# The fourth silu behind the next superstep's first two copies, and one weight tile 384 bytes further on

## The reference, cut to what matters

```python
g = jnp.einsum('bsh,ehf->ebsf', x, w_gate)      # x [2048, 256], e: 8 experts, f: 1024
u = jnp.einsum('bsh,ehf->ebsf', x, w_up)
h = jax.nn.silu(g) * u
expert_out = jnp.einsum('ebsf,efh->ebsh', h, w_down)
cw = router_probs * gate_weights                # softmaxes over the 8 experts
cw = cw / (jnp.sum(cw, axis=-1, keepdims=True) + 1e-09)
out = jnp.einsum('ebsh,bse->bsh', expert_out, cw)
```

## Time and profile before

| | us |
|---|---|
| median of 3 runs | 1723.94 |
| the three runs | 1719.41 to 1731.8 |
| the profiled execution, its own time | 1721.44 |
| its span, first to last instruction | 1719.6 |

### The profile page before, as it was taken

One profiled execution on the slowest core, in us unless ns is written; L12 is line 12 of the kernel. 1 busy time (PEld: TensorE's weight loads), 2 busy tenths in 40 slices (PEclk: granted clock), 3 DMA queues, 4 the chain that ended last, 5 costly groups with the idle time before them and its releaser, 6 DMA issues. The chain is left out here.

```text
span 1719.6 us, 25997 instructions
## 1 busy us (share of the span) xinstructions
PE 1578.9 (92%) x7985; PEld 1287.3 (75%) x7986; DVE 1205.1 (70%) x2226; ACT 874.0 (51%) x1548; POOL 665.8 (39%) x585
## 2 busy tenths in 40 slices
PE   6999986879993888889999999999999999999998
PEld 5796673368882777768888888778788788888787
DVE  6656878646665789567677777767767776876875
ACT  4455332134432456555665665665666655656653
POOL 2453156688806633330440530521612603604400
PEclk9998999889996999889999999999999999999999
DMA  6995012168843212000100100201101101101001
GB/s 198 264 328 207 13 69 93 62 211 260 253 138 112 80 36 74 1 1 27 56 31 31 56 13 31 68 0 49 49 0 49 49 1 56 42 12 55 31 13 50
DMA packets 74493, 136.38 MB, mean 79 GB/s; under 512 B 8592, under 2 KB 52176, under 8 KB 74256
## 3 DMA queue, kind: packets, MB, share of 16 engines
q1 hardware_dynamic: 40544, 92.76, 16.5%
q10 hardware_dynamic: 27696, 25.51, 4.8%
q0 software_dynamic: 6144, 16.79, 3.1%
HBM read 90.93 MB, written 44.11 MB: 79 GB/s over the span
## 5 line engine op out<-in xcount | busy, mean ns | idle before, releaser
L1356 DVE TENSOR_TENSOR gU<-ps,gU 128x512 f32<-128x512 f32 x384 | 256.7, 686 | 78.7 <-PE ps L2566 62.2
L2042 POOL TENSOR_TENSOR cL<-cR,cH 128x384 fp32r<-128x384 f32 x192 | 213.4, 1137 | 237.1 <-ACT cH L1734 237.1
L1349 DVE TENSOR_TENSOR eL<-eF,eH 128x512 fp32r<-128x512 f32 x256 | 190.0, 742 | 159.3 <-ACT eH L1829 159.3
L1813 ACT ACTIVATE gU<-ps 128x512 f32<-128x512 f32 x384 | 225.3, 596 | 124.4 <-PE ps L2566 110.1
L1829 ACT ACTIVATE eH<-eF 128x512 fp32r<-128x512 f32 x256 | 161.2, 630 | 162.9 <-DVE eF L1344 162.2
L2566 PE MATMUL ps<-xTH,cH 128*128 128x512 f32 x512 | 203.6, 398 | 10.2 <-DVE eF L1344 5.7
L2566 PE MATMUL ps<-xTL,cH 128*128 128x512 f32 x512 | 201.6, 394 | 0.0
L2566 PE MATMUL ps<-xTH,cL 128*128 128x512 f32 x512 | 201.4, 393 | 0.0
L2586 PE MATMUL ps<-eH,cL 128*128 128x512 f32 x480 | 189.1, 394 | 0.0
L2586 PE MATMUL ps<-eH,cH 128*128 128x512 f32 x480 | 188.5, 393 | 0.0
L2029 POOL TENSOR_TENSOR cR<-cR 128x256 f32<-128x256 f32 x32 | 34.1, 1064 | 395.2 <-DMA cR<-in_w 395.2
(11 more groups left out here) (439 smaller groups left out, 3447.3 us busy)
## 6 DMA issues: line engine op xcount, KB each, us to landing
cR<-in_w SPq DMA_DIRECT2D x32, 768.0 KB, 4.2
slots_in<-eS SPq DMA_DIRECT2D x16, 768.0 KB, 10.4
eS<-in_wr SPq DMA_DIRECT2D x32, 384.0 KB, 4.3
xl<-slots_in ACTq DMA_DIRECT2D x48, 256.0 KB, 3.8
slots_out<-yo ACTq DMA_DIRECT2D x48, 256.0 KB, 3.4
cwB<-expert_weights SPq DMA_DIRECT2D x16, 512.0 KB, 3.6
k_parts<-parts SPq DMA_DIRECT2D x8, 512.0 KB, 4.7
q_parts<-parts SPq DMA_DIRECT2D x8, 512.0 KB, 3.9
```

Source lines behind the costliest of these rows:

```text
L1349: dve.tensor_tensor(eL[:, b, :], eF[:, b, :], f32(eH[:, b, :]), ALU.subtract).then_inc(block_low, 1)
L1356: dve.tensor_tensor(to[:, :], ps[:, 2 + half, :], to[:, :], ALU.add).then_inc(half_summed, 1)
L1813: act.activation(to[:, :], ps[:, half, :], ACT.Identity).then_inc(snap_done, 1)
L2042: last = pool.tensor_tensor(cL[c][:, cols_], cR[c][:, cols_], f32(cH[c][:, cols_]), ALU.subtract)
```

## The change

In ScalarE's order the silu of the fourth inner block leaves the end of its superstep. It is issued in the next superstep, behind the two copies of k = 0 and right ahead of that block's `high_of`; behind the last superstep it stands alone. And `cH[3]` begins 384 bytes later, at byte 163840; it now reaches 384 bytes into `cw2`, and `cwc` moves to the second half of `cw2`. No instruction is added or removed.

```diff
-        cwc = at("cwc", [P, E1, NT], F32, start["cw2"])
+        cwc = at("cwc", [P, E1, NT], F32, start["cw2"] + 512)
...
-                                         (start["wS"] + 8 * CW, start["wS"] + 12 * CW), (start["sc0"], start["dcw"] + 8 * CW))):
+                                         (start["wS"] + 8 * CW, start["wS"] + 12 * CW), (start["sc0"] + 384, start["dcw"] + 8 * CW))):
...
-        assert end["cL2"] <= end["wL"] and end["cH3"] <= end["selm"] and end["cL0"] == start["cL3"]
+        assert end["cL2"] <= end["wL"] and end["cH3"] <= start["cwc"] and end["cwc"] <= end["cw2"] and end["cL0"] == start["cL3"]
...
+                before = (e, s - 1) if s else (e - 1, STEPS - 1)
                 snapshot(e, s, 0, 0)
                 snapshot(e, s, 0, 1)
                 if not start:
-                    high_of(*((e, s - 1) if s else (e - 1, STEPS - 1)), 3)
+                    gate(*before, 3)
+                    high_of(*before, 3)
...
                 high_of(e, s, 2)
                 if first and s == 2:
                     exponentials()
-                gate(e, s, 3)
...
             expert(E1 - 1, last=True)
+            gate(E1 - 1, STEPS - 1, 3)
             high_of(E1 - 1, STEPS - 1, 3)
```

## The result

The changed kernel takes 1731.91 us (median of 14 runs, 1727.75 to 1738.93) beside 1722.18 for the kernel before (14 runs, 1716.19 to 1731.8): a ratio of 1.0063, 95% interval 1.0046 to 1.008. It is slower by 0.6% where 5.6 us of gain were forecast, and it lies above the range of 1707 to 1728. Its profiled execution has a span of 1727.7 us, 8.1 more than that of before.

The account below looks back on a forecast made before the run. The prediction took TensorE's pace, and the few places where it waits, to bound the dense stage. Costs of 1.4 + 3.4 + 1.6 less a gain of 12.0 made minus 5.6, from 1721.44 to 1716 us, range 1707 to 1728.

Parts of the forecast that it names:

- (a): In 28 supersteps with a chunk, P7 waits for ScalarE's later copies of k = 1: 0.05 us each, 1.4 us.
- What comes: Part following the later silu: `hidden` 3 starts at about 2.75 us after the first matmul; three places have less slack.
- the loop's turn: VectorE's turn in superstep 0 of pass 6, after which `hidden` 3 came only at 2.68 us.
- this slack hides it: In a plain superstep the move costs nothing: `hidden_rest` 3 ends at 4.8 us, ahead of 5.18.
- Rival 2: In 28 supersteps with a chunk, `hidden` 3 meets GpSimd, lasts 1.2 us or more, P7 waits: 1728 to 1729; chance 0.1.
- The address: Chunk 3's high part on a multiple of 1024 bytes brings slow supersteps to 14.96 us: a gain of 12.0 us.
- Rival 1: The place isn't what slows chunk 3, the shift does nothing and only costs are left: 1728 us; chance 0.12.
- `add_out` in the last pass: P2 waits for VectorE's later `add_out` in four supersteps: 0.95 us in three, 0.55 in superstep 2, 3.4 in all.
- The existing stalls: TensorE's weight waits in supersteps 1 and 2 of passes 2 to 5: number unchanged, 1.6 us more taken.
- Rival 3: The moved silu dissolves the stalls of supersteps 1 and 2, and P7's wait is covered: 1708 us; chance 0.13.

Follow-up runs that it names:

- place_only: The kernel before with only chunk 3's high part at the new place, the silu at its old one: 1712.87 us, ratio 0.9959.
- place_128: The kernel before with chunk 3's high part 128 bytes later, `cwc` in the second half of `cw2`: 1713.28 us.
- silu_only: The changed kernel with chunk 3's high part at its old place, so only the silu's new order: 1734.43 us, ratio 1.0061.
- pass_edge_old: The changed kernel with superstep 7's fourth silu at its old place, ahead of each pass's end: 1733.38 us, ratio 1.0067.
- place_written_out: The kernel before with the new place and VectorE's passes 2 to 6 written out, the silu in old order: 1705.34 us, ratio 0.9935.
- load_later: The changed kernel with SyncE issuing chunk 2's load of 768 KB one unit later: 1724.95 us, ratio 1.0011.

## Why the prediction was wrong

**The step that failed** is (a) of "What comes", the wait of P7 in the 28 supersteps with a chunk, taken at 0.05 us each, 1.4 in all. In 24 of them it is of the right kind and small: with the loop written out the weights wait 20 times, 4.4 us in all, and such supersteps, where nothing else disturbs them, last 14.99 to 15.07. In the other four, superstep 0 of passes 3 to 6, it was 16.6 us. That is most of the distance between the 5.6 us of gain forecast and the 13.9 of loss in the dense stage. The step took "the loop's turn" at 2.68 as a fixed time and even as its nearest row for the price; the plain-superstep sentence "this slack hides it" then looked only at TensorE's and VectorE's own waits in superstep 7. It followed `high_of` 3 to `hidden_rest` 3 and the copies, but not through the chunk's third to silu 0 and GpSimd, and from there to the end of VectorE's pass. A tenth that VectorE loses there has nothing to hide it at the faster pace: in `place_only`, without the silu's move, `hidden` 3 behind the turn starts at 2.93 in pass 6 and at 3.24 in pass 4, and these supersteps 0 last 15.22 and 15.52 instead of 14.96. The rows had it already: an idle time of 2.04 that ended on "issue" led to copies that ended just ahead of P7's first weights.
The page "SBUF — State Buffer" of the Trainium skill, section "Who interferes with whom", says that a VectorE instruction with two inputs in SBUF contends with GpSimd instructions that read it. The trace agrees: with GpSimd at work `hidden` takes 0.80 to 1.35 us, and 0.69 at 1447.09 with none.

**Rival 2** had the right symptom, P7 waiting for ScalarE by more than half a microsecond, and a wrong cause: `hidden` 3 isn't stretched where the rival put it (0.69 us at 1447.09), it is kept back by the turn.

**The address** was right: the same 66 matmuls take 14.96 us at the new place for every chunk, 9.5 us less in the 39 others of the table. With what it saved in the rest it comes to 11.9, against 12.0: the 7.5 that `place_only` gained, the 2.6 and 0.2 that its supersteps 1, 2 and 0 lost, and the 0.35 and 1.24 (seven times 0.05, four times 0.31) that they would have gained by the pace. **Rival 1** is ruled out. What spoke for it, slow units with chunk 2's weights in superstep 7 (391 to 396 ns in pass 1 before), went with the place: 389 in `place_only`. The rule that the prediction set against the place, from the page "SBUF — State Buffer" of the Trainium skill, section "Who interferes with whom", of independent ports for data and weights that never wait, would have made all places alike; the traces disagree, 15.39 us at one place and 14.96 at another 128 bytes away (`place_128`).

**`add_out` in the last pass** was right: +2.9 us, and +3.3 beside the faster pace of `place_only` (69.86 against 66.52), where 3.4 was forecast; against `place_only` it is 0.96 in superstep 3, 0.91 in 6 and 7, and 0.55 in 2, where 0.55 was only a value taken between 0 and 0.95, so that this one is luck. In superstep 3 (from 1634.20; compare):

```profile
1638.37 0.69 DVE L1349 TENSOR_TENSOR eL<-eF,eH 128x512 fp32r<-128x512 f32 x1 [0.70 <-ACT eH L1829]
1638.97 1.28 DVE L1391 TENSOR_TENSOR x<-ps,x 128x512 f32<-128x512 f32 x2
...
1640.31 0.19 PEld L2568 LDWEIGHTS ps<-xTH,cH 128*128 128x128 f32 x1 [1.40 <-DVE x L1391]
```

P2's wait is 1.40 instead of 0.43: 0.97 more, against 0.95.

**The existing stalls** were mis-sized: 1.6 was taken, within bounds of 5 either way, and supersteps 1 and 2 lost 4.4. (The 1.6 doesn't quite follow from its own terms either: 0.4 and 0.2 for each of the seven supersteps that stalled before are 1.8.) Each part alone costs there: `place_only` 2.6 without any move of the silu, `silu_only` 4.0 at the old pace. The two overlap, so that no share of the 4.4 belongs to one of them; that TensorE at the faster pace comes sooner to places where VectorE has no time left is the likely reason of the 2.6, and isn't shown. **Rival 3** is ruled out by the same column.

**What stays open:** why pauses of the same length brought the clock down in passes 4 to 6 and not in 3, and in passes 3 to 5 and not in 6 in `pass_edge_old` (18.08 us there); the shares of silu 0 and GpSimd; and why supersteps 2 still stall in `place_written_out`. No run here takes these apart.

## What to carry to other kernels

When an instruction moves later, follow every engine that its queue feeds, to the end of the pass: here the silu's delay went through ScalarE's queue and GpSimd to the end of VectorE's pass. An engine's loop turn is work on the path like any other, with a start, a length and a DMA behind it; if a row shows idle time that ends on "issue", ask what the queue carries at that moment and how much later the turn may come. A move that frees time where nothing waits can only cost: the fastest kernel here keeps the silu at its old place. And two gains or losses that meet at one point don't add, so run the parts alone as well as together.

## What the runs showed of the hardware that I had not expected

- The turn of VectorE's loop took 2.04 us from its last instruction to its next in pass 6 of the kernel before and 3.79 in the changed kernel, where its instruction packet came among those of a 768 KB load; with the load a little later, 2.3.
- A weight tile 128 bytes past a multiple of 256 cost up to 0.43 us per 66 matmuls (15.39 against 14.96), at three such places; at two multiples of 256 it cost nothing.
- After pauses of 2.6 to 2.8 us without a matmul the granted clock fell to the lower level in six of eight cases (three of four in the changed kernel, three of four in `pass_edge_old`), and the superstep lost 1.5 us to that beside the pause; after pauses of 1.3 to 1.7 us (`silu_only`) and 1.0 to 1.2 (`load_later`) it did not.
